# Transposing half of the context by DMA, with a scale for every context row, in a gated cross-attention and expert kernel

## The reference

```python
x = x + tanh(g_xattn) * (gelu(layernorm(x) @ ctx.T) @ ctx)       # per batch, ctx is 750 x 512
xf = layernorm(x); scores = softmax(xf @ gate_w)                   # 8 experts, the best 2 of each row
h = silu(scale * xf @ w1) * (scale * xf @ w3)                      # HID = 256
x = x + tanh(g_ffn) * sum over experts of h @ w2
```

## Time and profile before

| | |
|---|---|
| median of three runs | 888.49 us (888.43 to 896.68) |
| the profiled execution's own time | 896.77 us |
| its span, first to last instruction | 895.0 us |
| mean granted TensorE clock | 0.912 of 2.4 GHz |
| busy share of the span | PE 79%, PEld 54%, ACT 52%, DVE 48%, POOL 42% |
| HBM | 61.89 MB read, 32.01 MB written, 105 GB/s over the span |

### The profile page before, as it was taken

How to read it: one execution, slowest core, us unless ns; L and a number is a source line. 1 busy time by engine, 2 the same in 40 slices (tenths; PEclk the granted TensorE clock), 3 DMA queues, 4 the chain that set the end, 5 groups by cost and what they waited for, 6 DMA issues and landing times.

```text
span 895.0 us, 17317 instructions
## 1 busy us (share of the span) xinstructions
PE 703.4 (79%) x4670; PEld 480.1 (54%) x4671; DVE 426.1 (48%) x1282; ACT 468.1 (52%) x771; POOL 378.7 (42%) x472
## 2 busy tenths in 40 slices
PE   0688888797878788887789316888898899888883
...
GB/s 121 116 71 185 121 99 130 132 127 106 102 161 127 102 116 146 126 106 106 160 102 65 65 1 60 95 100 100 94 94 94 106 106 106 94 99 103 94 103 70
DMA packets 61561, 94.22 MB, mean 105 GB/s; under 512 B 15872, under 2 KB 24192, under 8 KB 61536
## 3 DMA queue, kind: packets, MB, share of 16 engines
q1 hardware_dynamic: 45136, 60.03, 22.6%
...
HBM read 61.89 MB, written 32.01 MB: 105 GB/s over the span
## 4 chain that ended last, share of the span: by engine, by line
DMA 43%; issue 16%; PE 16%; DVE 8%; ACT 7%; POOL 6%; SPq 2%; POOLq 1%; DVEq 1%; ACTq 0%
DMA out_rows<-ctx_raw,meta 25%; DMA ctx_raw<-in_ctx 12%; PE bank L1125 8%; DMA meta<-route_table 3%; PE bank L1113 3%; POOL route_table L464 2%; PE bank L1070 2%; PE bank L1099 2%; DVE ctx_part L780 2%; ACT ctxT L591 1%; SPq L387 1%; ACT ctx_part L586 1%; DVE stats L758 1%; DVE a_part L789 1%; ACT w2s L620 1%
## 5 line engine op out<-in xcount | busy, mean ns | idle before, releaser
L1254 PE MATMUL bank<-w,ctxT 128*128 x756 | 175.6, 383 | 0.2 <-DVE ctxT L1025 0.2
L1125 PE MATMUL bank<-ctx_part,a_part 125*112 125x512 f16 x576 | 158.0, 427 | 12.1 <-DVE a_part L789 12.1
L1113 PE MATMUL bank<-xnT,ctxT 128*125 128x224 f16 x1152 | 131.8, 276 | 7.3 <-DVE xnT L810 7.3
L1113 PEld LDWEIGHTS bank<-xnT,ctxT 128*125 128x125 f16 x1152 | 123.4, 149 | 8.4 <-issue 7.9
L510 POOL DMA_INDIRECT ctx_raw<-xf_rows,meta x66 | 64.6, 979 | 141.3 <-issue 102.3
L522 POOL DMA_INDIRECT out_rows<-ctx_raw,meta x63 | 99.9, 1586 | 50.7 <-DMA out_rows<-ctx_raw,meta 24.3
L1254 PEld LDWEIGHTS bank<-w,ctxT 128*128 128x128 f16 x756 | 74.3, 98 | 77.1 <-issue 3.2
L1125 PEld LDWEIGHTS bank<-ctx_part,a_part 125*112 125x112 f16 x576 | 80.3, 145 | 61.9 <-issue 17.3
L591 ACT ACTIVATE ctxT<-bank 128x1000 f16<-128x1000 f16 x96 | 94.6, 1007 | 30.9 <-PE bank L1070 30.8
L1264 PE MATMUL bank<-w2s,ctxT 128*128 x378 | 91.9, 379 | 1.3 <-DVE ctxT L1030 1.3
L735 ACT ACTIVATE ctxT<-bank,cols 128x256 f32<-128x256 f32 x63 | 29.8, 473 | 115.0 <-issue 105.2
...
## 6 DMA issues: line engine op xcount, KB each, us to landing
...
meta<-route_table SPq DMA_DIRECT2D x66, 1.0 KB, 1.7
ctx_raw<-xf_rows,meta POOLq DMA_INDIRECT x66, 3.6
route_table<-route,pos_i POOLq DMA_INDIRECT x64, 4.7
```

The lines of the kernel that those rows point to most:

```text
L1113: ins = t_.matmul(dst, ctxT[u][:, hc * KD + k, c * CS:c * CS + CR], xnT[u][:, hx, k, :], start=j == 0, stop=j == KD * len(PARTS) - 1)
L1125: ins = t_.matmul(O_ps[t][0:TT, :], a_part[ha][:, c, t * TT:(t + 1) * TT], ctx_part[u][hc][:, c, :], start=c == 0 and (ha, hc) == PARTS[0] ...
L1254: ins = t_.matmul(H_ps[u][:, :], rows, w, start=m == 0, stop=m == KD * len(PARTS) - 1)
```

## The change

1. **A scale for each partition and third.** `ctx_s` and `ctx_inv` become three columns. POOL computes column q (`rows_scale`) straight from column q of `ctx_sum`, one step earlier than the old scale, and `ctx_high_part` waits for that instead of the common scale. The scale of the whole context (`all_s`) is still computed, from the same total, but only for the factors; a row's own scale is undone in `h_s` and `a_s`, which become three columns too. Three more chains of four POOL instructions per step.
2. **Low halves turned by DMA.** `turn_low` on SP issues a transposing DMA of one third of the low half (128 partitions by 1024 float16, 256 KB; three padding partitions are zeroed once at the start) into a part of `ctxT` of its own. It waits for `ctx_split` in the place where `load_ctx` of the same third waited, and stands just ahead of that load. `scores` waits for the landing (`lowT_ready`).
3. **High halves turned by PE.** `trans_ctx` and `ctxT_out` now take a third at once: 8 matmuls and one copy per third for the high half alone, three copies per step where there were six. They wait for `ctx_high` instead of `ctx_split`.
4. Small moves: the late weight total no longer waits for transposes, `Q` shares memory with `squares`.

The core of the diff (the reordered calls in `step` of PE and ACT are shown as order rows below it):

```diff
-A_BITS = -(D.bit_length() // 2)
+A_BITS = -(D.bit_length() // 4 + 1)
 
...
-        ctxT_buf = [sb(f"ctxT{u}", [P, 2 * KD * NC * CS], F16) for u in range(2)]
-        ctxT = [b[:, :].rearrange("p (g c) -> p g c", g=2 * KD) for b in ctxT_buf]
+        ctx_part = [[sb(f"ctx_part{u}{h}", [(CR, P)[h], NC, D], F16) for h in range(2)] for u in range(2)]
+        highT, lowT = NC * KD * CS, NC * KD * P
+        ctxT_buf = [sb(f"ctxT{u}", [P, highT + lowT], F16) for u in range(2)]
+        ctxT = [[b[:, 0:highT].rearrange("p (g c) -> p g c", g=NC * KD), b[:, highT:highT + lowT].rearrange("p (g c) -> p g c", g=NC * KD)] for b in ctxT_buf]
         squares = [sb(f"squares{n}", [P, KD * HID], F16) for n in range(2)]
+        Q = squares[0][:, 0:2 * E * 3].bitcast(F32)
         ctx_sum = sb("ctx_sum", [P, NQ])
         ctx_gsum = sb("ctx_gsum", [P, NQ])
         ctx_max = sb("ctx_max", [P, 1])
         exp_f = sb("exp_f", [P, 2])
         exp_i = exp_f[:, 1:2].bitcast(I32)
-        ctx_s = [sb(f"ctx_s{u}", [P, 1], I32) for u in range(2)]
-        ctx_inv = [sb(f"ctx_inv{u}", [P, 1], I32) for u in range(2)]
-        tanh_a = sb("tanh_a", [P, 1])
-        factors = sb("factors", [P, 6])
-        a_s = [factors[:, u:u + 1] for u in range(2)]
-        h_s = [factors[:, 2 + u:3 + u] for u in range(2)]
-        o_s = [factors[:, 4 + u:5 + u] for u in range(2)]
+        ctx_s = [sb(f"ctx_s{u}", [P, NQ], I32) for u in range(2)]
+        ctx_inv = [sb(f"ctx_inv{u}", [P, NQ], I32) for u in range(2)]
+        all_s, all_inv = sb("all_s", [P, 1], I32), sb("all_inv", [P, 1], I32)
+        factors = sb("factors", [P, 2, 2 * NQ + 1])
+        a_s = [factors[:, u, 0:NQ] for u in range(2)]
+        h_s = [factors[:, u, NQ:2 * NQ] for u in range(2)]
+        o_s = [factors[:, u, 2 * NQ:2 * NQ + 1] for u in range(2)]
         x_sb = [sb(f"x{u}", [TT, 2, D]) for u in range(2)]
...
@@ -307,6 +310,12 @@
                 sp.dma_start(ctx_raw[0:CR, 2 * q:2 * q + 2, :],
                              ctx[bass.ds(i * C + 2 * q * CR, 2 * CR), :].rearrange("(c p) d -> p c d", p=CR)).then_inc(ctx_loaded[q], 16)
 
+            def turn_low(i, u, q):
+
+                hold(sp, ctx_split, i * NQ + q + 1)
+                sp.dma_start_transpose(ctxT[u][1][:, 2 * q * KD:(2 * q + 2) * KD, :],
+                                       ctx_part[u][1][:, 2 * q:2 * q + 2, :].rearrange("p c d -> p (c d)")).then_inc(lowT_ready[u][q], 16)
+
             def load_weight(n, kind, e):
...
@@ -347,16 +356,18 @@
                     store_rows(i - 1)
                     if not last:
                         load_x(i + 1, 1 - u)
-                if load_two:
-                    for q in range(NQ - 1):
-                        sp.wait_ge(ctx_split, i * NQ + (NQ + q + 1))
+                for q in range(NQ - 1):
+                    if not last:
+                        turn_low(i + 1, 1 - u, q)
+                    if load_two:
                         load_ctx(i + 2, q)
                 if not u and later(i, 1):
                     first_matrix(load_weight, i, u, h)
                 if later(i, 1):
                     store_norm(i - 1)
+                if not last:
+                    turn_low(i + 1, 1 - u, NQ - 1)
                 if load_two:
-                    sp.wait_ge(ctx_split, i * NQ + 2 * NQ)
                     load_ctx(i + 2, NQ - 1)
                 second_matrix(load_weight, i, u, h)
...
 
                 seq.done(g.tensor_scalar(exp_i, gmax.bitcast(I32), 0.5 ** (MANT + 1), None, ALU.mult))
                 seq.hold()
                 seq.done(g.tensor_scalar(exp_f[:, 0:1], exp_i, float(ROOT), float(1 << MANT), ALU.add, ALU.mult))
                 seq.hold()
-                seq.done(g.tensor_scalar(inv, exp_f[:, 0:1], float((TOP - 1) << MANT), None, ALU.subtract))
-                return g.tensor_scalar(s, exp_f[:, 0:1], -1.0, float((2 * BIAS + TOP - 1) << MANT), ALU.mult, ALU.add)
-
-            def context_scale(i, u):
+                seq.done(g.tensor_scalar(inv, exp_f[:, 0:1], float((TOP - 1 + bits) << MANT), None, ALU.subtract))
+                return g.tensor_scalar(s, exp_f[:, 0:1], -1.0, float((2 * BIAS + TOP - 1 + bits) << MANT), ALU.mult, ALU.add)
+
+            def rows_scale(i, u, q):
+
+                hold(pool, ctx_sum_ready, i * NQ + q + 1)
+                scale_from(ctx_sum[:, q:q + 1], ctx_inv[u][:, q:q + 1], ctx_s[u][:, q:q + 1]).then_inc(ctx_scaled, 1)
+
+            def context_scale(i):
 
                 hold(pool, ctx_gsum_ready, i + 1)
                 seq.done(g.tensor_scalar(ctx_max[:, :], ctx_gsum[:, 0:1], ctx_gsum[:, 1:2], ctx_gsum[:, 2:3], ALU.max, ALU.max))
                 seq.hold()
-                scale_from(ctx_max[:, :], ctx_inv[u][:, :], ctx_s[u][:, :]).then_inc(ctx_scaled, 1)
+                scale_from(ctx_max[:, :], all_inv[:, :], all_s[:, :], A_BITS).then_inc(all_scaled, 1)
 
             def weight_scale(n, kind, e):
...
                 if not u:
                     first_matrix(weight_scale, i, u, h)
                 if later(i, 2):
                     exps(i - 2)
+                if two:
+                    rows_scale(i + 2, u, 2)
                 if last:
                     send_routes(i - 2, u)
 
...
-                if q == 0 and later(i, 1):
+                if later(i, 1):
+                    act.wait_ge(ctx_scaled, i * NQ - NQ + q + 1)
                     act.wait_ge(ctx_tot_made, i)
                 a.activation(squares[0][0:CR, :].rearrange("p (c d) -> p c d", c=2), ctx_raw[0:CR, 2 * q:2 * q + 2, :], ACT.Square,
...
 
                 act.wait_ge(w_tot_made, n + 1)
                 if later(n, 1):
                     act.wait_ge(w_scaled, n)
-                a.activation(w_gsum[:, :], w_tot[b], ACT.Copy).then_inc(w_gsum_ready, 1)
-
-            def late_tot_out(n, kind, e):
-
-                weight_tot_out(n, kind, e, 1)
+                a.activation(w_gsum[:, :], w_tot, ACT.Copy).then_inc(w_gsum_ready, 1)
 
             def ctx_high_part(i, u, q):
-                if q == 0:
-                    act.wait_ge(ctx_scaled, i + 1)
-                    if later(i, 2):
-                        act.wait_ge(attn_part, i * NQ - NQ)
+                act.wait_ge(ctx_scaled, i * NQ + q + 1)
+                if q == 0 and later(i, 2):
+                    act.wait_ge(attn_part, i * NQ - NQ)
                 c = slice(2 * q, 2 * q + 2)
-                a.activation(ctx_part[u][0][:, c, :], ctx_raw[0:CR, c, :], ACT.Copy, scale=ctx_s[u][0:CR, :].bitcast(F32)).then_inc(ctx_high, 1)
-
-            def ctxT_out(i, u, c):
-
-                act.wait_ge(ctxT_made, i * NC + c + 1)
-                a.activation(ctxT[u][:, :, c * CS:c * CS + CR], T_half[c % 2], ACT.Copy).then_inc(ctxT_ready, 1)
+                a.activation(ctx_part[u][0][:, c, :], ctx_raw[0:CR, c, :], ACT.Copy, scale=ctx_s[u][0:CR, q:q + 1].bitcast(F32)).then_inc(ctx_high, 1)
+
+            def ctxT_out(i, u, q):
+
+                act.wait_ge(ctxT_made, i * NQ + q + 1)
+                a.activation(ctxT[u][0][:, 2 * q * KD:(2 * q + 2) * KD, 0:CR], T_half[(u + q) % 2], ACT.Copy).then_inc(ctxT_ready, 1)
 
             def gelu(i, u, q):
...
-                a.activation(a_f[m][:, :], H_ps[m][0:CR, 0:2 * S], ACT.Gelu_apprx_tanh, scale=h_s[u][0:CR, :]).then_inc(a_ready, 1)
+                a.activation(a_f[m][:, :], H_ps[m][0:CR, 0:2 * S], ACT.Gelu_apprx_tanh, scale=h_s[u][0:CR, q:q + 1]).then_inc(a_ready, 1)
                 act.wait_ge(a_ready, n + 1)
...
-                dve.wait_ge(ctx_scaled, i + 1)
+                dve.wait_ge(ctx_scaled, i * NQ + NQ)
+                dve.wait_ge(all_scaled, i + 1)
                 if later(i, 2):
                     dve.wait_ge(x2_ready, i * 2 - 2)
-                s, inv = ctx_s[u][:, :].bitcast(F32), ctx_inv[u][:, :].bitcast(F32)
-                seq.done(v.tensor_scalar(a_s[u][:, :], s, 2.0 ** A_BITS, None, ALU.mult))
-                seq.done(v.tensor_scalar(o_s[u][:, :], inv, inv, tanh_a[:, :], ALU.mult, ALU.mult))
-                v.tensor_scalar(h_s[u][:, :], inv, 2.0 ** -X_BITS, None, ALU.mult).then_inc(factors_ready, 1)
+                s, s_inv, inv = all_s[:, :].bitcast(F32), all_inv[:, :].bitcast(F32), ctx_inv[u][:, :].bitcast(F32)
+                seq.done(v.tensor_scalar(a_s[u], inv, s, s, ALU.mult, ALU.mult))
+                seq.done(v.tensor_scalar(o_s[u], s_inv, s_inv, g_tanh[:, 0:1], ALU.mult, ALU.mult))
+                v.tensor_scalar(h_s[u], inv, 2.0 ** -X_BITS, None, ALU.mult).then_inc(factors_ready, 1)
 
             def context_low(i, u, q):
 
                 dve.wait_ge(ctx_high, i * NQ + q + 1)
+                if q == 0 and not later(i, 2):
+                    dve.wait_ge(pad_made, i + 1)
                 c = slice(2 * q, 2 * q + 2)
-                v.scalar_tensor_tensor(ctx_part[u][1][:, c, :], ctx_raw[0:CR, c, :], ctx_s[u][0:CR, :].bitcast(F32), ctx_part[u][0][:, c, :],
```

(27 more changed lines are left out.)

88 lines of the change are left out of this document (39 added, 49 removed).

## The result

| | before | after |
|---|---|---|
| median | 890.1 us (4 runs, 888.4 to 896.7) | 921.2 us (4 runs, 918.9 to 924.5) |
| ratio | | 1.034, 95% interval 1.027 to 1.041 |
| the profiled execution | 896.8 us, span 895.0 | 923.5 us, span 921.8 |
| mean granted clock | 0.912 | 0.893 |

The forecast was 916 us, or +27.8 us from one profiled execution to the other; these two differ by 26.7 us, and the medians by 31 us. The kernel is slower, near the forecast. The steps behind that number are another matter, as the trace and twelve further kernels show. Where some runs of a kernel fell in a slower state of the chip (five of ten, in one kernel only), its median and ratio are those of the other runs.

The account below looks back on a forecast made before the run. Bound: first-stage landings, with loads queued on about five DMA engines. 25.9 for pairs of steps + 3.5 at the start - 1.6 at the end = +27.8 us, so 916 us beside the median; range 866 to 975.

Parts of the forecast that it names:

- The bound: First stage: no engine full; ACT waits for landings, whose loads of 125 partitions queue on about five DMA engines.
- the three waits named: ACT's waits for landings in a pair: weights 1.58 and 1.61 us, last context third 2.29 us; to grow 2 to 4 each.
- T: Time one transposing DMA holds each DMA engine: taken as 1.33 us, between 0.69 and 4.6.
- The issue on SP: Issuing a transposing DMA holds SP 0.28 us, like a load; a longer issue would be hidden behind the five engines' queue.
- 3T: Engine time of a step's three transposing DMAs queued ahead of its loads: 4.0 us.
- Even and odd step: Gelu after an even step's squares moves +0.8 us, an odd step costs +3.2; 6.5 pairs, +25.9 us.
- Start and end: Wait for batch 1's last third grows +3.5 us; at the end PE keeps its saved 1.6 us.
- POOL: Three added scale chains take 3.7 us per step on POOL; cost taken as 0, bounds -0.5 and +1.2 us a pair.
- PE and ACT: PE saves 1.56 us per batch, mostly covered by waits; ACT drops three 1.0 us copies per step, of which 0.9 us pays.
- The rival that this decides: Loads hide the transposing DMAs and PE's and ACT's saved work counts: -23 us, 865; chance 0.26.
- What I said would show it: First stage alone grows, landing waits grow, ctx_s wait goes, DMA share +0.13; over +0.3, or scores waiting for lowT_ready, means wrong.
- 6T: Engine time of a pair's six transposing DMAs: pair costs 6T - 4.0 = +4.0 us, DMA share rises 0.13.

Follow-up runs that it names:

- tiny DMAs: Changed kernel with a plain copy for each transposing DMA, plus three plain DMAs of one 256-byte row behind each copy: 924.5 us, ratio 1.040.
- the order on SP: Changed kernel with each transposing DMA issued behind the load of the same third instead of ahead of it: 890.9 us, ratio 0.994.
- Scale only: Kernel before plus the scale for each partition and third, both halves still transposed by PE: 883.3 us, ratio 0.994.
- without landings in the way: Context loads cut into 112 and 13 partitions: changed kernel 858.5 us, kernel before 864.0, kernel with the new scale but PE transposes 865.8.
- the DMAs behind the loads: Changed kernel with loads cut into 112 and 13 partitions and each transposing DMA issued behind its third's load: 853.4 us, ratio 0.958.

## Why the prediction was right, and where it was not

**The bound: right in kind.** Landings end both steps. Of the three waits named, only that for the last third in the even step grew (2.29 to 6.19 us); the even step's weight stayed (1.61 to 1.76). I had the weight end the odd step; it is the last third there too (4.68 us), and the weight's wait vanished behind it. The wait for `ctx_s` is gone, as said.

**T: sized 15% or more too high.** 1.33 us was taken, 0.91 to 1.16 measured. With 1.16 the sum is 6.5 x (6 x 1.16 - 4.0) + (3 x 1.16 - 0.5) - 1.6 = +20.6 us, and with 0.91 it is +10, both short of the 26.7. The steps that load a batch ahead are 14 (i = 0 to 13) and not 13, which adds half a pair, at most 1.5 us.

**The issue on SP: the step that failed.** "Its issue on SP I take at the 0.28 us of a load; a longer one would be hidden while the five engines have a queue." It takes 1.24 us and up to 4.06, and it was not hidden. Measured from its issue the load took no longer than before; its issue was 2.9 us later than before in the even step shown and 4.0 us in the odd, 3.4 us on average over the 14 steps. The shorter transfer gives 1.4 us of that back; that the load would have queued for this time anyway is likely, and not shown. The loss is not 3T of engine time but the issues ahead of each load: tiny DMAs that add only SP's time to plain copies cost all of it, and the order on SP takes it away. That the number was near is luck: it came from two errors that cancel, an engine time that the queue mostly hides, for an issue time that it doesn't.

**Even and odd step.** Forecast +0.8 and +3.2 us; the table has 2.6 / 7 = +0.4 and 17.9 / 7 = +2.6, together +20.5 us for the forecast's +25.9. The even step of the trace closes: from squares to squares 31.66 us before and 32.77 after, +1.1. The low half starts 2.0 us earlier and the load goes out 2.9 us later behind it (issue 19.2 and 20.0 us after the squares), and 0.3 us come with the transfer. So the earlier scale does in the even step what was said of it (2.3 us), against a delay of another kind than was said. With the old scale the same load is 4.8 us late on average, and the cost is 48 us.

**Start and end.** Start +3.5 forecast, +3.3 measured. End -1.6 forecast, nothing found: +3.0 for the end and the second stage, which was to stay level.

**POOL: 0 forecast, bounds up to +1.2 a pair; a wait outside them.** ACT's wait for w_s went from 4.6 to 25.1 us in the long window, some 2.8 us a pair, and between 60 and 480 us it is 20 to 29 us in every kernel with the new scale, for 1.4 before. Scale only is slightly faster even so. No run takes this wait away, so what it costs stays open.

**PE and ACT.** ACT is busy 5 us less in a pair where 6 were forecast, and PE 3 us less. The rival that this decides fell: without landings in the way the change, or its transposing DMAs alone, are worth 5 to 7 us (858.5 against 864.0 and 865.8), and some 10 us with the DMAs behind the loads (0.958 against 0.967 and 0.969, intervals that overlap), not 23.

**What I said would show it.** `scores` never waits for lowT_ready in the changed kernel, as said. The DMA share rose by 0.26 in a pair, twice the 0.13 of 6T and just under the 0.3 that was to mean a T too small, while T was too large. The share adds up the time of packets, also where they overlap (1.26 above), so a rise of it does not give T; a stretch with one transfer comes nearer.
